# Group sums of a normalisation: on VectorE by 32x32 transposes instead of TensorE products with a matrix of group means

## What is computed

```
xg = x.reshape(B, H, W, 32, C // 32)
xn = (xg - xg.mean((1, 2, 4))) * rsqrt(xg.var((1, 2, 4)) + EPS) * gamma + beta
q, k, v = xn @ wq + bq, xn @ wk + bk, xn @ wv + bv
out = softmax(q @ k.T / sqrt(C)) @ v @ wp + bp + x
```

## Time and profile before

| | |
|---|---|
| median of 3 runs | 252.61 us (252.58 to 252.69) |
| the profiled execution, its own time | 254.9 us |
| its span, first to last instruction | 253.1 us |
| VectorE busy | 187.3 us, 74% |
| ScalarE busy | 149.4 us, 59% |
| GpSimd busy | 125.2 us, 49% |
| granted TensorE clock | 1.00 |

### The profile page before, as it was taken

One profiled execution on the slowest core, in us unless ns is written; L12 is line 12 of the kernel. 1 busy time (PEld: TensorE's weight loads), 2 busy tenths in 40 slices (PEclk: granted clock), 3 DMA queues, 4 the chain that ended last, 5 costly groups with the idle time before them and its releaser, 6 DMA issues.

```text
span 253.1 us, 4585 instructions
## 1 busy us (share of the span) xinstructions
PE 247.7 (98%) x1570; PEld 225.3 (89%) x1570; DVE 187.3 (74%) x490; ACT 149.4 (59%) x291; POOL 125.2 (49%) x151
## 2 busy tenths in 40 slices
PE   8899999999999999999999999999999999999995
PEld 6698889889998899889998899889998899889995
DVE  0279899988995788677885898687875788448804
ACT  2466434499995407930998607940998609740930
POOL 3010260388488605911597925911697927800870
PEclk9999999999999999999999999999999999999999
DMA  6999000000025001320034001320010001100112
GB/s 187 329 181 212 9 0 3 0 1 3 0 84 83 4 0 44 83 42 3 22 84 65 0 0 44 84 42 3 28 57 3 0 0 44 41 0 3 43 41 85
DMA packets 34767, 12.37 MB, mean 49 GB/s; under 512 B 26284, under 2 KB 34488, under 8 KB 34744
## 3 DMA queue, kind: packets, MB, share of 16 engines
q1 hardware_dynamic: 34720, 12.07, 19.5%
q10 hardware_dynamic: 24, 0.01, 0.0%
HBM read 7.88 MB, written 4.19 MB: 48 GB/s over the span
## 4 chain that ended last, share of the span: by engine, by line
PE 89%; DVE 6%; DMA 2%; issue 1%; ACT 1%; SPq 0%; DVEq 0%
PE ring L1133 12%; PE ring L1135 12%; PE ring L1134 12%; PE ring L1108 10%; PE ring L1107 10%; PE ring L1109 10%; PE ring L1080 3%; PE ring L1082 3%; PE ring L1081 3%; PE ring L1093 3%; PE ring L1095 2%; PE ring L1094 2%; DMA xnat<-in_x 2%; PE ring L947 2%; DVE R L732 2%; DVE xraw L593 1%
## 5 line engine op out<-in xcount | busy, mean ns | idle before, releaser
L363 POOL TENSOR_TENSOR P_lo<-S,P_hi 128x512 fp32r<-128x512 f32 x64 | 81.9, 1304 | 52.0 <-ACT S L503 51.9
L1133 PE MATMUL ring<-V,P_hi 128*128 128x258 f32 x256 | 72.7, 284 | 0.0
L1135 PE MATMUL ring<-V,P_lo 128*128 128x258 f32 x256 | 72.4, 283 | 0.0
L1134 PE MATMUL ring<-V,P_hi 128*128 128x256 f32 x256 | 72.3, 282 | 0.0
L502 ACT ACTIVATE P_hi<-S 128x512 fp32r<-128x512 f32 x64 | 40.3, 630 | 29.8 <-DVE S L791 29.8
L495 ACT COPY S<-ring 128x512 f32<-128x512 f32 x64 | 36.6, 590 | 31.3 <-PE ring L1109 29.4
L1107 PE MATMUL ring<-t_hi,xn_lo 128*128 128x512 f32 x128 | 49.9, 390 | 0.0
L1108 PE MATMUL ring<-t_lo,xn_hi 128*128 128x512 f32 x128 | 49.8, 389 | 0.0
L1109 PE MATMUL ring<-t_hi,xn_hi 128*128 128x512 f32 x128 | 49.8, 389 | 0.0
L1133 PEld LDWEIGHTS ring<-V,P_hi 128*128 128x128 f32 x256 | 48.5, 189 | 0.4
L1134 PEld LDWEIGHTS ring<-V,P_hi 128*128 128x128 f32 x256 | 48.4, 189 | 0.4
(11 more groups left out here) (117 smaller groups left out, 360.7 us busy)
## 6 DMA issues: line engine op xcount, KB each, us to landing
xnat<-in_x SPq DMA_DIRECT2D x8, 256.0 KB, 4.6
between<-xnat SPq DMA_DIRECT2D x16, 128.0 KB, 1.8
out<-xnat SPq DMA_DIRECT2D x16, 128.0 KB, 1.7
moved<-in_x SPq DMA_DIRECT2D x8, 128.0 KB, 4.4
moved<-between SPq DMA_DIRECT2D x16, 64.0 KB, 2.3
moved<-between SPq DMA_DIRECT2D x32, 32.0 KB, 1.9
w_wq<-in_L_conv_wq SPq DMA_DIRECT2D x2, 256.0 KB, 4.7
w_wk<-in_L_conv_wk SPq DMA_DIRECT2D x2, 256.0 KB, 4.6
```

The costliest lines, as they stand in the source:

```text
L363: nc.gpsimd.tensor_tensor(P_lo[:, exp_of(c, kb), :], S[:, tile_of(c, kb), :], P_hi[:, exp_of(c, kb), :].bitcast(F32), ALU.subtract).then_i ...
L1133: nc.tensor.matmul(bank[:, 0:C + 2], P_hi[:, tile, mine], v[:, kb, 0:C + 2], start=(kb == 0), stop=False)
L1134: nc.tensor.matmul(bank[:, 0:C], P_hi[:, tile, mine], v[:, kb, C + 2:VX], start=False, stop=False)
L1135: last = nc.tensor.matmul(bank[:, 0:C + 2], P_lo[:, tile, mine], v[:, kb, 0:C + 2], start=False, stop=(kb == NB - 1))
```

## The change

The mean and variance of each channel of units 1 to 3 are written as two of 64 columns of `mv_turn` (the others are zero). A 32x32 transpose puts the channels of a partition block into columns (`turned`): 4 groups of 8 neighbours. VectorE reduces the groups, subtracts the mean, squares, adds the variances, reduces again, and a second transpose with broadcast input brings both sums back to the channels' partitions. The two matrix products of these units, their ring tiles M and G and their waits are gone. Unit 0 is as before. `shift_to_all(0)` stands behind V product 6 instead of 5. The semaphore `dv_stat` counts 15 steps for a later unit instead of 11.

```
-    ring_order += [("V", 0, 0), ("M", 1)]
-    ring_order += [("V", 0, m) for m in range(1, 4)]
-    ring_order += [("G", 1)]
-    ring_order += [("V", 0, m) for m in range(4, NB)]
+    ring_order += [("V", 0, 0)]
+    ring_order += [("V", 0, m) for m in range(1, NB)]
...
+            def turn_statistics(v):
+                dve.wait_ge(dv_stat, stat(v, 0, AGGR_D))
+                nc.vector.transpose(turned[:, :, :].rearrange("p n c -> p (n c)"),
+                                    mv_turn[:, :, :].rearrange("p n c -> p (n c)")).then_inc(dv_stat, 1)
+                dve.wait_ge(dv_stat, stat(v, 0, TURN_D))
+                nc.vector.tensor_reduce(group_sums[:, 0, :], means, AX_X, ALU.add).then_inc(dv_stat, 1)
+            def turned_deviation(v):
+                nc.vector.scalar_tensor_tensor(means, group_sums[:, 0, :, None].to_broadcast([P, QB, PER_GROUP]),
+                                               -1.0 / PER_GROUP, means, ALU.mult, ALU.add).then_inc(dv_stat, 1)
+                nc.vector.tensor_tensor(means, means, means, ALU.mult).then_inc(dv_stat, 1)
+                nc.vector.tensor_tensor(variances, variances, means, ALU.add).then_inc(dv_stat, 1)
+            def turned_variance(v):
+                nc.vector.tensor_reduce(group_sums[:, 1, :], variances, AX_X, ALU.add).then_inc(dv_stat, 1)
+                nc.vector.transpose(sums_back[...], group_sums[...][:, :, None].to_broadcast(
+                                        [P, 2 * QB, PER_GROUP])).then_inc(dv_stat, 1)
+                nc.vector.tensor_scalar(var_e[:], sums_back[:, 1, 0:KC], 1.0 / PER_GROUP,
+                                        eps[:, v // IMAGES:v // IMAGES + 1], ALU.mult, ALU.add).then_inc(dv_stat, 1)
...
-            group_deviation(1)
             for m in range(QB):
                 v_low(0, m)
...
             query_shift(0)
-            variance(1)
+            turn_statistics(1)
             for m in range(QB, NB):
                 v_low(0, m)
+                if m == QB:
+                    turned_deviation(1)
+                if m == QB + 1:
+                    turned_variance(1)
                 if m < NB - 1:
                     attention_vector(1, m - QB)
...
                     channel_statistics(u + 1)
+                    turn_statistics(u + 1)
                 running_max(second, 7)
                 if more:
-                    group_deviation(u + 1)
+                    turned_deviation(u + 1)
+                    turned_variance(u + 1)
...
             for m in range(NB):
                 values(0, m)
-                if m == 0:
-                    mean_of_groups(1)
                 if m == 2:
                     maxima_by_query(0)
-                if m == 3:
-                    variance_of_groups(1)
-                if m == 5:
+                if m == 6:
                     shift_to_all(0)
```

More of the change, by code:

```diff
@@ L91, in two_attention_layers @@
         if u < UNITS - 1:
-            ring_order += [("O", 2 * u, 0), ("M", u + 1), ("O", 2 * u, 1), ("G", u + 1)]
-            ring_order += [("O", 2 * u, j) for j in range(2, QB)]
+            ring_order += [("O", 2 * u, j) for j in range(QB)]
             ring_order += [("t", u + 1, 0, k) for k in range(KC)]
@@ L147, in two_attention_layers @@
         gmean = sb("gmean", [P, KC])
+        mv_turn = sb("mv_turn", [P, 2, SQ])
+        turned = sb("turned", [P, 2, SQ])
+        group_sums = sb("group_sums", [P, 2, QB])
+        sums_back = sb("sums_back", [P, 2, SQ])
         dev = sb("dev", [P, KC])
@@ L249, in mean_bank, with stat @@
         def mean_bank(v):
-            return ring[RING - 1][:, C:C + KC] if v == 0 else bank_of("M", v)[:, 0:KC]
+            return ring[RING - 1][:, C:C + KC]
         def variance_bank(v):
-            return ring[RING - 1][:, C:C + KC] if v == 0 else bank_of("G", v)[:, 0:KC]
+            return ring[RING - 1][:, C:C + KC]
         AGGR, DEV, DEV2, VARC, VARE, R0SQ, RERR, RSTD, GAIN, GMUL, SHIFT = range(1, 12)
-        STAT = SHIFT
+        (AGGR_D, TURN_D, GSUM_D, DEV_D, DEV2_D, VARC_D, GVAR_D, BACK_D, VARE_D, R0SQ_D, RERR_D, RSTD_D, GAIN_D, GMUL_D,
+         SHIFT_D) = range(1, 16)
+        def stat(v, first, later):
+            return first if v == 0 else SHIFT + (v - 1) * SHIFT_D + later
         def count_R(c, kb):
@@ L575, in _ @@
             nc.vector.memset(minus_half[:], -0.5)
+            nc.vector.memset(mv_turn[:], 0.0)
             for v in V:
@@ L636, in channel_statistics, with group_deviation @@
                 for k in range(KC):
-                    last = nc.vector.bn_aggr(mv[:, k, :], bn[:, k, :, :].rearrange("p b s -> p (b s)"))
+                    last = nc.vector.bn_aggr(mv[:, k, :] if v == 0 else mv_turn[:, :, k],
+                                             bn[:, k, :, :].rearrange("p b s -> p (b s)"))
                 last.then_inc(dv_stat, 1)
[L640 to L646, removed]
+            def group_deviation():
+                dve.wait_ge(pe_gm, 1)
+                nc.vector.tensor_copy(gmean[:], mean_bank(0))
+                dve.wait_ge(dv_stat, AGGR)
+                nc.vector.tensor_tensor(dev[:], mv[:, :, 0], mean_bank(0), ALU.subtract).then_inc(dv_stat, 1)
+                dve.wait_ge(dv_stat, DEV)
@@ L647, in group_deviation, with variance @@
                 nc.vector.tensor_tensor(dev2[:], dev[:], dev[:], ALU.mult).then_inc(dv_stat, 1)
-                dve.wait_ge(dv_stat, at + DEV2)
+                dve.wait_ge(dv_stat, DEV2)
                 nc.vector.tensor_tensor(var_c[:], dev2[:], mv[:, :, 1], ALU.add).then_inc(dv_stat, 1)
[L651 to L654, removed]
+            def variance():
+                dve.wait_ge(pe_gv, 1)
+                nc.vector.tensor_scalar(var_e[:], variance_bank(0), eps[:, 0:1], None, ALU.add).then_inc(dv_stat, 1)
@@ new lines, in _ @@
+            means, variances = (turned[:, n, :].rearrange("p (g j) -> p g j", j=PER_GROUP) for n in range(2))
+            def turn_statistics(v):
[4 more added lines that the diff above has]
+                nc.vector.tensor_reduce(group_sums[:, 0, :], means, AX_X, ALU.add).then_inc(dv_stat, 1)
@@ new lines, in turned_variance @@
+            def turned_variance(v):
+                dve.wait_ge(dv_stat, stat(v, 0, VARC_D))
+                nc.vector.tensor_reduce(group_sums[:, 1, :], variances, AX_X, ALU.add).then_inc(dv_stat, 1)
+                dve.wait_ge(dv_stat, stat(v, 0, GVAR_D))
+                nc.vector.transpose(sums_back[:, :, :].rearrange("p n c -> p (n c)"),
+                                    group_sums[:, :, :].rearrange("p n g -> p (n g)")[:, :, None].to_broadcast(
+                                        [P, 2 * QB, PER_GROUP])).then_inc(dv_stat, 1)
+                dve.wait_ge(dv_stat, stat(v, 0, BACK_D))
+                nc.vector.tensor_scalar(var_e[:], sums_back[:, 1, 0:KC], 1.0 / PER_GROUP,
+                                        eps[:, v // IMAGES:v // IMAGES + 1], ALU.mult, ALU.add).then_inc(dv_stat, 1)
@@ L693, in _ @@
             channel_statistics(0)
-            group_deviation(0)
+            group_deviation()
             A_low(0, 0)
-            variance(0)
+            variance()
             A_low(0, 1)
@@ L883, in statistics_again @@
                     if more:
-                        variance(u + 1)
                         affine_map(u + 1)
@@ L1012, in wait_for_bank, with mean_of_groups, variance_of_groups @@
                     pe.wait_ge(dv_R, count_R(*at))
[L1014 to L1026, removed]
+            def mean_of_groups():
+                pe.wait_ge(ac_xT, 4)
+                pe.wait_ge(dv_stat, AGGR)
+                nc.tensor.matmul(mean_bank(0), group_mean[:], mv[:, :, 0], start=True, stop=True).then_inc(pe_gm, 1)
+            def variance_of_groups():
+                pe.wait_ge(dv_stat, VARC)
+                nc.tensor.matmul(variance_bank(0), group_mean[:], var_c[:], start=True, stop=True).then_inc(pe_gv, 1)
             def keep_running(n):
@@ L1138, in attend, with attention @@
                     last.then_inc(pe_O, 1)
-            def attention(c, behind, statistics=False):
+            def attention(c, behind):
                 pe.wait_ge(po_P, (c + 1) * NB)
@@ L1209, in _ @@
                     scores(second, kb)
-                attention(first, {3: next_first_half}, more)
+                attention(first, {3: next_first_half})
             for kb in range(BY_KEYS):
```

38 lines of the change are left out of this document (18 added, 20 removed).

## The result

The changed kernel takes 250.82 us (median of 6 runs, 250.40 to 251.29), beside 252.67 for the kernel before (6 runs): a ratio of 0.9922, 95% interval 0.9901 to 0.9943. Forecast was 251.1 in 250.7 to 252.0. By the medians 1.85 us went; by the ratio, 252.61 x 0.9922 = 250.64, 1.97 us went, which is just past the near edge. A later comparison on another chip (`e1_after`) gave 0.9928 [0.9913, 0.9943]: 1.42 us by the medians, 252.23 against 250.81, and 1.82 us by the ratio. 251.1 / 252.61 = 0.9940 lies in both intervals. Of all runs in this document only two of the six of e12 are slower ones, 255.13 and 255.62 us at a granted clock of 0.987, and its numbers leave them out.

What follows compares the result with a forecast made beforehand. TensorE, busy 98%, was taken to bound the kernel; 0.64 us from unit 1 and 0.88 from units 2 and 3 make 1.52 less, from 252.61 to 251.1 us. Own range 250.8 to 251.5; 8 in 10, 250.7 to 252.0.

Steps and rivals of the forecast that it cites:

- Bound: TensorE, busy in 98% of the span: its work plus its few stalls set the end.
- Products: Six group_mean products leave TensorE in units 1 to 3, 0.22 us each, 1.33 us in all.
- Rival (c): Most of a product's 0.22 us on TensorE stays, each gives only 0.05; total 252.1 us; chance 0.04.
- The move: Spreading the shift behind V product 6 removes TensorE's 0.24 us stall at its transposes.
- The new chain: Eight small VectorE instructions in each of units 1 to 3 add 1.59 us a unit.
- Rival (a): VectorE's small steps cost 0.05 us more each, 0.40 a unit; total 251.9 us; chance 0.17.
- rival (b): VectorE's 64-column transposes cost about what 512 do, 0.92 us more a unit; total 253.5, slower; chance 0.06.
- Unit 1: VectorE's chain to the outputs moves 0.64 us earlier, so this unit brings 0.64 us.
- (d): VectorE's chain is 0.1 to 0.3 us shorter, TensorE alone holds unit 1; 250.95 us; chance 0.68 together with the forecast.
- Units 2 and 3: Both keep TensorE's 0.44 us, 0.88 together, with x_low leads on GpSimd of 0.12 and 0.22 us left.
- the last of the sum: Carries the profile's saving of 1.52 us over to the median of runs, 252.61, giving 251.1 us.

Runs made afterwards that it cites:

- e1_after: The changed kernel again, no edit, timed against the kernel before on another chip; 250.81 us, ratio 0.9928.
- e12: e7 once more, unchanged, timed against the kernel before; ratio 0.9923, four runs of 250.26 to 251.51 us.
- e11: Changed kernel with six unread 2-column group_mean products put back among V products of units 0 to 2; 252.52 us (one run).
- e8: Changed kernel without VectorE's group sums and deviations in units 1 to 3, each channel using its own statistics; 250.46 us, ratio 0.9922.
- e2: Kernel before with only the shift moved from behind V product 5 to behind V product 6; 252.05 us, ratio 0.9987.
- e3: Changed kernel with the shift back behind V product 5; 250.77 us, ratio 0.9941 to the kernel before.
- e6: Changed kernel with an 832-column reduce behind var_e in units 1 to 3, keeping VectorE 0.92 us; 253.31 us, ratio 1.0035.
- e7: Changed kernel with all four outputs of chunk 0 ahead of both low t splits of chunk 1 on VectorE; 250.22 us, ratio 0.9916.
- e5: Changed kernel with a 320-column reduce behind var_e in units 1 to 3, keeping VectorE 0.39 us; 251.63 us, ratio 0.9977.
- e10: e7 with unit 1's affine map moved behind the maximum of block 3 of chunk 1; 252.32 us, ratio 0.9993 to the kernel before.
- e9: e5 with one more memset of 64 columns at the start of VectorE's program; 251.44 us (one run).

## Why the prediction was right, and where not

**Bound: right.** TensorE's work and its few stalls set the end. e11 puts the products back, and the stretch grows by their price; e8 takes most of the new work off VectorE and gains 0.05.

**Products: right, slightly high.** 0.213 us each against 0.22. Rival (c), 0.05 each, is refuted, and with it the price worked out from the Trainium skill's page "TensorE: Matmul & The Clock Gate" (section "Wait — 56ns, not 53.3ns?"): start-to-start near 25 ns isn't what a small product costs between two weight loads of others. The page gives it as a floor, which 0.213 us doesn't contradict. That the neighbours' weight loads are the reason, as the prediction has it, no run tested by itself.

**The move: right.** 0.24 forecast; 0.27 in e2 and 0.22 in e3.

**The new chain: right.** 1.56 against 1.59 us, transposes 0.24 to 0.25 against 0.26. Rival (a) asked for 0.05 more a step, rival (b) for 0.46 more a transpose; neither came. What (b) said would follow from such a price is real, as e6 shows: slower than before, by 1.04 us in the stretch, beside 0.90 in (b).

**Unit 1: 0.69 against 0.64.** TensorE gained 0.76 and gave back 0.07 at the fourth V product. The prediction had two limits close together for the second exponential, 50.80 by VectorE's chain and 50.76 by TensorE. It came at 48.48 + 2.27 = 50.75, and e8 puts TensorE's limit 0.05 earlier: near tie and order are right. What was wrong is the gain that (d) promised to a shorter chain, 0.04 and 0.10 from the stall at the fourth V product: in e8 that stall stays at 0.12, since the output's place behind a t split holds it (e7), and only 0.05 comes.

**Units 2 and 3: 0.46 and 0.41 against 0.44 each.** About kept in full. By the rows the leads of x_low were 0.19 and 0.01 to 0.03, against 0.12 and 0.22: unit 3 held with next to nothing to spare, which is partly luck. A chain somewhat longer would still have cost little there, since TensorE's matmuls follow their weight loads: e5's 0.39 us cost each of the two units 0.12.

**The step that failed is the last of the sum:** "The median of the runs shown is 252.61, 2.3 below that execution, and the same microseconds are gone from it: 251.1." As a middle it holds: the medians fell by 1.42 and 1.85 us in two comparisons, 1.64 on average, and the stretch with the remainder by 1.66. As a range it doesn't. The near edge, 250.7, left 0.4 us on that side. The only reason named for that side was (d), which reaches 250.95 and didn't come, and nothing stood for the part ahead of the first t product, which in the profiles starts anywhere from 18.1 to 21.2 us, nor for the 0.10 us of the remainder. Medians of a few runs carry some of that start: before's are 252.23 to 252.67 in five comparisons, after's 250.81 and 250.82. Of the 1.97 us by the ratio, 1.56 are the stretch (0.04 more than the 1.52 of the sum), 0.10 the remainder, 0.19 the estimated difference of the median starts in these runs, and 0.12 what the ratio of all runs has over that of the medians. Nothing shows the last two to be the change's: in e1 the estimated starts differ by 0.24 the other way, and over all comparisons they agree. So, as far as the runs tell, chance took the result past the edge, and the step that failed is to have carried the profile's sum over to the median with no term for the start and the remainder. That before's profiled execution was itself 2.3 above the median was read and used for the sum, but not for the range.

**Not named.** The chain was priced without GpSimd. e10 shows small VectorE steps of the same kind at 1.29 in place of 0.16 us beside P_lo. The new steps escape, since GpSimd stands idle while they run. In unit 1 its row before the power says so,

```profile
44.66 0.81 POOL L354 TENSOR_TENSOR r<-var_e,minus_half 128x2 f32<-128x2 f32 x1 [11.12 <-DVE var_e L690]
```

for 11 us; in units 2 and 3 it is 9.7. In e10 two steps that met P_lo cost 1.73 us of the stretch, more than the change brings. The affine map of unit 1 ends at 47.84 in the changed kernel, and P_lo starts at 48.29.

**Open.** The gap of 0.37 us that wanders with VectorE's program. The 0.10 us of the remainder, and how much of the varying start is the landing of the loads. Whether e7 beats after: by the stretch it does, 0.21 us in both of its profiles; by the times their intervals overlap.

## What to carry to other kernels

With an engine busy to 98%, price what leaves it by the start-to-start of its neighbours, and measure the others' leads. A delay of known length in the other engine's chain shows which leads count; the lead itself is read from the rows, since here 0.2 to 0.26 us of a weight load's wait cost the matmuls only 0.12. Cut a profiled execution where the steady work begins: here the stretch behind that repeated to 0.01 us in two pairs of profiles, where whole runs differed by 2 us, and the part ahead belongs in the range of the time. Before small steps go to VectorE, look at what GpSimd runs beside them.

## What the runs showed of the hardware

- A two-column VectorE step with two SBUF inputs was held for the whole of GpSimd's 128x512 instruction: 1.29 us in place of 0.16, twice in e10. GpSimd's 32x8 copies ran beside the same steps in the changed kernel with no such effect (0.15 to 0.17 us a step).
- One pair of dependent VectorE instructions, the reciprocal and the output behind it, starts 0.61 to 0.64 us apart in place of 0.26 once in each of five profiles (before, e2, e5, e6, e9). The place moves with the number of instructions ahead of it. In the other nine profiles none of the 32 pairs has it.
- In the changed kernel 32x32 transposes of 128x64 take 0.238 to 0.246 us, those of 128x512 0.70 to 0.73: about 1.06 ns a column over 0.18, near a small step's own 0.16.
- A 2-column fp32 product put between V products costs TensorE 0.213 us (e11, six of them).
